# Where a decoder layer splits its experts' weights into fp16 halves

## The chip, the cores and the metric

One core of one Trainium2 chip runs the whole layer in a single launch. The metric is the device time of the launch in microseconds. The engines are PE (TensorE, with its weight loads as PEld), DVE (VectorE), ACT (ScalarE), POOL (GpSimd) and SP (SyncE, which here only issues DMAs).

## The reference, cut to what matters

```python
x = x + attn(layernorm(x))                  # x: 32 x 64 x 256; 16 heads of 16, ternary weights, activations quantized to int8
x = x + xattn(layernorm(x), ctx)            # 16 heads of 128; q and k go through an rmsnorm; ctx: 32 x 64 x 128
logits = xf @ router_w.T                    # 8 experts, the best 2 per token, softmax of the two
g = einsum('th,efh->etf', xf, gate_w)       # F = 688
u = einsum('th,efh->etf', xf, up_w)
y = einsum('etf,ehf->eth', silu(g) * u, down_w)
out = x + einsum('te,eth->th', combine, y)
```

The kernel multiplies fp32 numbers as pairs of fp16 numbers: a high half, and a low half that is what the high half leaves. Each product then is three fp16 products (high by high, high by low, low by high). The experts' weights (gate, up and down of 8 experts, 34304 fp32 columns on 128 partitions with padding) must be turned into such halves before the experts run. This splitting does not depend on the activations, so it can be done anywhere before them; the change moves it.

## The kernel before, in words

The kernel is four blocks in a row, with a barrier of all engines between them. Within a block every engine runs its own list of instructions in order, and semaphores tie the lists together. A wait holds everything behind it on its engine.

`self_attention` (L73) first normalizes, quantizes and transposes, then does 16 rounds, one for each tile of 128 tokens (`attention_rounds`, L139; the order within a round is the `attend` function of each engine, at L266 for ACT, L401 for DVE, L502 for PE). In round t ACT copies the turned probabilities out of PSUM (L270), copies q and k of tile t+3 (`highs`, L248), copies the values of tile t (`values`, L239), takes the exponentials of tile t+1 (L277), and at the end does `split(t + 2)` (L254): it scales one sixteenth of the experts' weights by 64 in place (L261) and rounds them to their high halves (L263, L264). DVE does `lows(t + 2)` (L362), `scores(t + 1)` (L369, with the subtraction of the maximum at L382), `sums(t)` (L384) and `outputs(t - 1)` (L392). PE does `probs` (L490), `project` (L454), `values` (L482), `scores` (L472) and `outputs` (L498). POOL subtracts to get the low halves (L203, L205). SP loads the next fp32 sixteenth and saves the finished halves to `gu_pair` and `d_pair` in DRAM (L163 to L184). Of the splitting, 16 pieces of 2144 columns are done, one per round, two of them ahead of round 0.

`attention_output` (L534) projects the result, and prepares the operands of the cross-attention: `hT` (the turned hidden states), `cT` (the turned context), `wq`, `wk`, `wvo`, `ck`.

`cross_attention` (L781) works on 4 groups of 512 tokens with 16 heads each, two heads per step: 32 pairs. It is written out step by step, `steps` N = -9 to 32 (L817). At step N the pair N+9 is projected (`query`, `key`, `squares`), the pair n = N+1 gets its scores and softmax, and pair N is attended and projected out. So steps -9 to -2 only project, steps -1 to 22 do all three, and the last steps, from N = 23, have no projection left. In a step, ACT's order is (L910 to L942): `out_high` of the odd head before (L893), `norm_logs` where a group opens, `query` (L882, L883), the copy of the turned probabilities pT (L922), the exponentials (L925), `key` (L889), `out_high` of the even head, `query` again, the cast of the probabilities (L937), `key` again. POOL's is (L860 to L874): multiply by the reciprocal sums (L869), multiply the next pair's norms (`both_norms`, L858), subtract for the low half of the probabilities (L874). PE turns that low half only when it is there (L1076). Where a group opens (n = 0, 8, 16, 24), ACT takes logs and exponentials of the norms (L897, L901, each with a load of its function table), SP writes them to DRAM and reads them back spread over the partitions in 16 DMAs (L847), and POOL and DVE wait for that. ACT issues no DMA in this block.

`experts` (L1160) routes the tokens, and runs 39 slots of 128 tokens on their experts, with the halves loaded back by SP (L1264, L1265). The loads of the first three experts are issued at its start, and those of the others once the routing is done.

Of the kernel before, what the change touches and what calls it, by code (L numbers as in the profile page):

```python
# [5 lines left out]
F32 = mybir.dt.float32  # L6
# [10 lines left out]
P = 128  # L17
# [51 lines left out]
GU, DH = NCH * FF, FT // 2 * C  # L69
CHUNK = GU + DH  # L70


def self_attention(nc, sem, dram, x_sb, cst, ao, arena):  # L73
# [4 lines left out]
    with ctx:  # L78
# [40 lines left out]

        raw = [arena[:, i * CHUNK:(i + 1) * CHUNK] for i in range(2)]  # L120
        pair = [arena[:, i * CHUNK:(i + 1) * CHUNK].bitcast(F16) for i in (2, 3)]
        raw_in = [sem(f"raw_in{i}") for i in range(2)]
        raw_zero, raw_scaled, pair_high, pair_low = sem("raw_zeroed"), sem("raw_scaled"), sem("pair_high"), sem("pair_low")
        pair_out = [sem(f"pair_out{i}") for i in range(2)]

# [28 lines left out]
        with nc.Block() as block:  # L154

            @block.sync
            def _(sp_):
# [5 lines left out]
                def load(e, g):  # L163
                    sp_.dma_start(raw[g][:, 0:GU], dram["wgu"][bass.ds(e, 1), g].rearrange("a p n -> (a p) n")).then_inc(raw_in[g], 16)
                    wd = dram["wd"][bass.ds(e, 1)]
                    full = 3 - g
                    sp_.dma_start(raw[g][:, GU:GU + full * C].rearrange("p (k o) -> p k o", o=C),
                                  wd[:, g * 3 * P:(g * 3 + full) * P, :].rearrange("a (k p) o -> p (a k) o", p=P)).then_inc(raw_in[g], 16)
                    if g:
                        sp_.dma_start(raw[g][0:FL, GU + 2 * C:GU + 3 * C], wd[:, (FT - 1) * P:FF, :].rearrange("a p o -> (a p) o")).then_inc(raw_in[g], 16)  # L170

                def save(e, g):
                    sp_.wait_ge(pair_low, e * 4 + 2 * g + 3)
                    sp_.dma_start(dram["gu_pair"][bass.ds(e, 1), :, g].rearrange("a p n -> (a p) n"), pair[g][:, 0:2 * GU]).then_inc(pair_out[g], 16)
                    sp_.dma_start(dram["d_pair"][bass.ds(e, 1), :, g].rearrange("a p n -> (a p) n"), pair[g][:, 2 * GU:2 * CHUNK]).then_inc(pair_out[g], 16)
                sp_.wait_ge(raw_zero, 1)
                load(0, 0)
                load(0, 1)
# [1486 lines left out]
```

## Time and profile before

| | us |
|---|---|
| device time, median of 3 runs | 1134.67 |
| lowest and highest of them | 1129.13, 1136.54 |
| the profiled execution, its device time | 1132.77 |
| its span, first to last instruction | 1131.0 |
| busy in the span: PE, DVE, ACT, POOL | 785.1, 674.0, 557.0, 342.8 |
| mean granted clock of PE, share of full | 0.877 |

The profiled execution is one of its own, 1.9 us below the median of the runs, and 1.8 us longer than its span. Matmul ends are modelled, and a share of busy time over the whole span mixes stages with different limits, so the rows below are read stage by stage.

### The profile page before, as it was taken

What the parts mean: (1) busy time and instruction counts of PE and PEld (TensorE: products, weight loads), DVE (VectorE), ACT (ScalarE), POOL (GpSimd) and SP (SyncE); (2) the same over time, 40 slices, a digit from 0 to 9 for tenths busy, and PEclk for the clock granted to TensorE, in tenths of its full rate; (3) what the DMA queues carried; (4) which work ended last, traced back from release to release, by engine and by line L of the source; (5) the groups of instructions that cost most, each with busy time, mean ns of one, the idle gap of its engine ahead of it and who ended that gap; (6) DMA issues with size and microseconds to landing.
All of it is one profiled execution on the core that took longest, in us unless ns stands there. A gap on an engine that the chain in (4) does not pass through costs nothing. (4 is left out here: it accounts for less than half of the span.)

```text
span 1131.0 us, 27058 instructions
## 1 busy us (share of the span) xinstructions
PE 785.1 (69%) x10378; PEld 562.7 (50%) x10379; DVE 674.0 (60%) x1178; ACT 557.0 (49%) x843; POOL 342.8 (30%) x375
## 2 busy tenths in 40 slices
PE   0015677752436769988997995665359999999993
PEld 0014666641322335655655664555346666666662
DVE  4996788869754557767776774546643333333330
ACT  0146899963733446555565654342124444444441
POOL 0301445532500013223232322330033444444442
PEclk9997776765758989998999997996569999999997
DMA  4002677648000020011002002007347222222223
GB/s 136 0 0 76 244 254 253 245 159 305 0 0 1 1 77 2 3 32 47 2 3 77 2 3 77 2 2 264 119 186 256 37 37 37 37 37 37 37 32 93
DMA packets 40062, 90.86 MB, mean 80 GB/s; under 512 B 5264, under 2 KB 25488, under 8 KB 38128
## 3 DMA queue, kind: packets, MB, share of 16 engines
q1 hardware_dynamic: 29168, 76.22, 19.0%
q0 software_dynamic: 7488, 10.23, 5.7%
q10 hardware_dynamic: 3328, 3.28, 0.8%
q8 instruction: 60, 0.98, 0.4%
q14 instruction: 18, 0.15, 0.0%
HBM read 62.71 MB, written 29.10 MB: 81 GB/s over the span
## 5 line engine op out<-in xcount | busy, mean ns | idle before, releaser
L1470 DVE SCALAR_TENSOR_TENSOR hid<-psu,hid 128x688 f32<-128x688 f32 x39 | 34.1, 874 | 168.4 <-ACT hid L1334 168.4
L1029 PE MATMUL xbank_q<-arena 128*128 128x512 f16 x384 | 97.7, 392 | 16.3 <-DVE q_hl L956 11.1
L1110 PE MATMUL xbank_a<-arena,x_o 128*128 128x256 f16 x768 | 96.2, 276 | 14.3 <-DVE x_o L966 14.3
L869 POOL TENSOR_TENSOR x_pf<-x_sc,x_rden 128x512 f32<-128x512 f32 x32 | 33.3, 1042 | 204.8 <-DVE x_rden L989 204.8
L1334 ACT ACTIVATE hid<-psg 128x688 f32<-128x688 f32 x39 | 29.0, 743 | 134.6 <-PE psu L1537 134.6
L1537 PE MATMUL psg<-wgu,f_xT 128*128 x468 | 76.6, 314 | 16.8 <-issue 10.9
L882 ACT ACTIVATE sqq<-xbank_q 128x512 f32<-128x512 f32 x64 | 38.2, 596 | 101.6 <-PE xbank_q L1029 101.6
L1551 PE MATMUL fbank<-arena,hidT 128*128 (+1 forms) x702 | 87.1, 273 | 1.5 <-ACT f_y L1352 0.8
L1110 PEld LDWEIGHTS xbank_a<-arena,x_o 128*128 128x128 f16 x768 | 73.0, 99 | 29.8 <-DVE x_o L966 21.2
L858 POOL TENSOR_TENSOR ao<-ao,rec_q 128x512 f32<-128x512 f32 x32 | 33.8, 1057 | 137.6 <-DMA ao<-key_norms 137.6
L1537 PE MATMUL psu<-wgu,f_xT 128*128 x468 | 75.0, 310 | 0.0
L956 DVE TENSOR_TENSOR q_hl<-xbank_q,q_hl 128x512 f16<-128x512 f32 x64 | 44.0, 687 | 47.4 <-ACT q_hl L883 47.4
L1551 PEld LDWEIGHTS fbank<-arena,hidT 128*128 128x128 f16 (+1 forms) x702 | 63.4, 97 | 16.9 <-issue 10.5
L203 POOL TENSOR_TENSOR arena<-arena 128x1376 f16<-128x1376 f32 x16 | 45.4, 2840 | 85.4 <-ACT arena L264 85.4
L1309 POOL DMA_INDIRECT token_out<-f_y,f_to x39 | 62.6, 1605 | 17.4 <-issue 17.0
L966 DVE SCALAR_TENSOR_TENSOR x_o<-xbank_o,x_o 128x512 f16<-128x512 f32 x64 | 43.9, 686 | 38.4 <-ACT x_o L893 38.3
L1537 PEld LDWEIGHTS psg<-wgu,f_xT 128*128 128x128 f16 x468 | 43.1, 99 | 47.0 <-issue 27.5
L1037 PE MATMUL xbank_k<-cT,wk 128*128 128x512 f16 x192 | 53.3, 388 | 12.9 <-DVE k_hl L962 12.9
L1029 PEld LDWEIGHTS xbank_q<-arena 128*128 128x128 f16 x384 | 33.0, 100 | 57.2 <-DVE q_hl L956 15.3
L893 ACT ACTIVATE x_o<-xbank_o 128x512 f16<-128x512 f32 x64 | 38.2, 597 | 40.4 <-PE xbank_o L1097 40.1
L1537 PEld LDWEIGHTS psu<-wgu,f_xT 128*128 128x128 f16 x468 | 46.0, 98 | 22.9
L960 DVE TENSOR_SCALAR k_hl<-xbank_k,x_gains 128x512 f16<-128x512 f32 x64 | 47.8, 747 | 10.7 <-ACT sqk L889 10.7
(278 smaller groups left out, 1932.0 us busy)
## 6 DMA issues: line engine op xcount, KB each, us to landing
arena<-in_wgu SPq DMA_DIRECT2D x16, 688.0 KB, 5.8
gu_pair<-arena SPq DMA_DIRECT2D x16, 688.0 KB, 3.1
wgu<-gu_pair SPq DMA_DIRECT2D x8, 1376.0 KB, 9.4
ao<-key_norms SPq DMA_DIRECT2D x64, 128.0 KB, 3.2
d_pair<-arena SPq DMA_DIRECT2D x16, 384.0 KB, 3.8
arena<-d_pair SPq DMA_DIRECT2D x8, 768.0 KB, 10.7
arena<-in_wd SPq DMA_DIRECT2D x8, 384.0 KB, 5.6
x_sb<-in_x SPq DMA_DIRECT2D x2, 1024.0 KB, 9.4
```

The source lines that it names most:

```text
L203: nc.gpsimd.tensor_tensor(pair[g][:, GU:2 * GU], raw[g][:, 0:GU], pair[g][:, 0:GU], ALU.subtract).then_inc(pair_low, 1)
L882: nc.scalar.activation(sqq[h % 2][:, :], bank_q[:, :], ACT.Square, scale=1.0 / (H_UP * W_UP)).then_inc(sq_done, 1)
L893: nc.scalar.mul(o_hl[h % 2][:, 0, :].rearrange("p (b n) -> p b n", b=2), ob[:, :, 0:RW], 1.0 / P_UP).then_inc(oh_done, 1)
L956: nc.vector.tensor_tensor(q_hl[:, 1, slot(h), :], bank_q[:, :], q_hl[:, 0, slot(h), :], ALU.subtract).then_inc(lq_done, 1)
L960: nc.vector.tensor_scalar(k_hl[:, 0, slot(h), :], bank_k[:, :], gains[:, 2:3], None, ALU.mult).then_inc(hk_done, 1)
L966: nc.vector.scalar_tensor_tensor(out=o_hl[h % 2][:, 1, :].rearrange("p (b n) -> p b n", b=2), in0=ob[:, :, 0:RW], scalar=1.0 / P_UP, in1=o ...
L1029: last = nc.tensor.matmul(bank_q[:, :], wq[:, a, k, f:f + D2], hT[:, b * NCH + k, at:at + GN], start=(j == 0), stop=(j == len(terms) - 1))
L1037: last = nc.tensor.matmul(bank_k[:, :], wk[:, a, f:f + D2], cT[:, b, at:at + GN], start=(j == 0), stop=(j == 2))
L1110: last = nc.tensor.matmul(acc[t // 2][:, (t % 2) * C:(t % 2 + 1) * C], o_hl[h % 2][:, a, at:at + P], wvo[:, b, e, :], start=(e == 0 and j ...
L1309: nc.gpsimd.indirect_dma_start(out=dram["token_out"], out_offset=bass.IndirectOffsetOnAxis(ap=to[:, 0:1], axis=0), in_=y[r ^ 1][:, :], in_ ...
L1537: last = nc.tensor.matmul(bank[:, c * 512:c * 512 + FH], xT[r][:, b * NCH + k, :], wgu[:, bass.ds(e, 1), at:at + FH].rearrange("p a n -> p ...
L1551: last = nc.tensor.matmul(ps[1][:, 0:C], hidT[r][0:rows, a, f, :], wd[0:rows, bass.ds(e, 1), at:at + C].rearrange("p a n -> p (a n)"), sta ...
```

## The change

The splitting is taken out of the self-attention rounds, of ACT, POOL and SP, and put into the steps of the cross-attention, on ACT and POOL. The weights now come in one array `wx` of 128 x 34304 fp32, in 67 pieces of 512 columns, two in each step from n = 0 to 33 (only one in the last). ACT itself issues the load of a piece (256 KB) and the save of its two halves (256 KB in 256 runs of 1 KB), where SP did before. ACT makes the high half in one operation straight from the fp32 piece (`piece_high`). POOL scales the piece in place, and subtracts (`piece_low`, two operations of 512 columns). There are two buffers: they lie in the parts of `hT` and `cT` that belong to group 0, which is why these two are laid out by group now, and why ACT issues the first two loads only at the end of step -2, when group 0 has been projected. `piece_save(i)` waits for POOL's low half, saves, and issues the load of piece i+2. At the end ACT waits for the last saves. The halves are kept in DRAM as one array `w_hl`, so the experts' loads read two runs per partition in place of one, with other offsets in `wgu` and `wd`. The copies to `hT` at L637 and L700 are written out in place of a loop.

```diff
@@ -66,8 +66,10 @@
 NE, FF = 8, 688
 FT = -(-FF // P)
 FL = FF - (FT - 1) * P
-GU, DH = NCH * FF, FT // 2 * C
-CHUNK = GU + DH
+GUC, DC = 2 * NCH * FF, FT * C
+EC = GUC + DC
+PIECE = 512
+NPIECE = NE * EC // PIECE
 
 
 def self_attention(nc, sem, dram, x_sb, cst, ao, arena):
...
-                def load(e, g):
...
-                def save(e, g):
-                    sp_.wait_ge(pair_low, e * 4 + 2 * g + 3)
...
-                with sp_.Fori(0, NE - 1) as e:
-                    for g in range(2):
-                        save(e, g)
-                        load(e + 1, g)
...
-                with pool.Fori(0, NE) as e:
-                    for g in range(2):
-                        pool.wait_ge(pair_high, e * 4 + 2 * g + 2)
...
-                        nc.gpsimd.tensor_tensor(pair[g][:, GU:2 * GU], raw[g][:, 0:GU], pair[g][:, 0:GU], ALU.subtract).then_inc(pair_low, 1)
...
-                        nc.gpsimd.tensor_tensor(pair[g][:, 2 * GU + DH:2 * CHUNK], raw[g][:, GU:CHUNK], pair[g][:, 2 * GU:2 * GU + DH], ALU.subtract).then_inc(pair_low, 1)
...
-                def split(t, r):
...
-                    act.wait_ge(raw_in[r], arrived)
...
-                    nc.scalar.mul(raw[r], raw[r], W_UP).then_inc(raw_scaled, 1)
-                    act.wait_ge(raw_scaled, t + 1)
-                    nc.scalar.copy(pair[r][:, 0:GU], raw[r][:, 0:GU]).then_inc(pair_high, 1)
-                    nc.scalar.copy(pair[r][:, 2 * GU:2 * GU + DH], raw[r][:, GU:CHUNK]).then_inc(pair_high, 1)
...
-                    if tile_there(t, 2):
-                        split(t + 2, r)
...
+        raw = [hT[:, 0].rearrange("p j n -> p (j n)").bitcast(F32)[:, i * PIECE:(i + 1) * PIECE] for i in range(2)]
+        pair_hl = [cT[:, 0], sb("x_pair", [P, 2, PIECE], F16)[:, :, :]]
+        raw_in, pair_out = [sem(f"x_raw_in{i}") for i in range(2)], [sem(f"x_pair_out{i}") for i in range(2)]
+        high_done, up_done, low_done = sem("x_pair_high"), sem("x_piece_up"), sem("x_pair_low")
         steps = range(-AHEAD, NPAIR + 1)
+
+        def piece(i):
+            return 0 <= i < NPIECE
 
         def pair(n):
             return 0 <= n < NPAIR
@@ -857,8 +808,17 @@
                     rq = rec_q[:, :, 2 * u:2 * u + 2].rearrange("p t h -> p h t").unsqueeze(3).to_broadcast([P, 2, GT, S])
                     nc.gpsimd.tensor_tensor(rk, rk, rq, ALU.mult).then_inc(rqk_done, 1)
 
+                def piece_low(i):
+                    r = i % 2
+                    pool.wait_ge(high_done, i + 1)
+                    nc.gpsimd.tensor_scalar(raw[r], raw[r], W_UP, None, ALU.mult).then_inc(up_done, 1)
+                    pool.wait_ge(up_done, i + 1)
+                    nc.gpsimd.tensor_tensor(pair_hl[r][:, 1, :], raw[r], pair_hl[r][:, 0, :], ALU.subtract).then_inc(low_done, 1)
+
                 for N in steps:
                     n = N + 1
+                    if piece(2 * n):
+                        piece_low(2 * n)
                     if opens(n):
                         both_norms(n)
                     if pair(n):
@@ -872,6 +832,8 @@
                         pool.wait_ge(ph_done, n + 1)
                         pool.wait_ge(pf_done, n + 1)
                         nc.gpsimd.tensor_tensor(p_hl[n % 2][:, 1, :], pf[:, :, :].rearrange("p a s -> p (a s)"), p_hl[n % 2][:, 0, :], ALU.subtract).then_inc(pl_done, 1)
+                    if piece(2 * n + 1):
+                        piece_low(2 * n + 1)
 
             @block.scalar
             def _(act):
@@ -906,11 +868,31 @@
                         act.wait_ge(rqk_done, g * NU)
                     nc.scalar.activation(rec_q[:, :, :].rearrange("p t h -> p (t h)"), bank_n[:, 2 * P:3 * P], ACT.Exp, scale=-0.5, bias=gains[:, 4:5]).then_inc(rq_done, 1)
 
+                def piece_load(i):
+                    act.dma_start(raw[i % 2], dram["wx"][:, i * PIECE:(i + 1) * PIECE]).then_inc(raw_in[i % 2], 16)
+
+                def piece_high(i):
+                    r = i % 2
+                    act.wait_ge(raw_in[r], (i // 2 + 1) * 16)
+                    if i >= 2:
+                        act.wait_ge(pair_out[r], i // 2 * 16)
+                    nc.scalar.mul(pair_hl[r][:, 0, :], raw[r], W_UP).then_inc(high_done, 1)
+
+                def piece_save(i):
+                    act.wait_ge(low_done, i + 1)
+                    act.dma_start(dram["w_hl"][:, :, i * PIECE:(i + 1) * PIECE].rearrange("l p n -> p l n"), pair_hl[i % 2]).then_inc(pair_out[i % 2], 16)
+                    if piece(i + 2):
+                        piece_load(i + 2)
+
                 act.wait_ge(g_ready, 4)
                 for N in steps:
                     n, m = N + 1, N + AHEAD
                     if head(2 * N - 1):
                         out_high(2 * N - 1)
+                    if piece(2 * n - 1):
+                        piece_save(2 * n - 1)
+                    if piece(2 * n):
+                        piece_high(2 * n)
                     if opens(n):
                         norm_logs(n // NU)
                     if pair(m):
@@ -927,6 +909,8 @@
                         key(2 * m)
                     if pair(N):
                         out_high(2 * N)
+                    if piece(2 * n):
+                        piece_save(2 * n)
                     if pair(m):
                         query(2 * m + 1)
                     if opens(n):
@@ -940,6 +924,18 @@
                     if opens(n):
                         act.wait_ge(pf_done, n + 1)
                         nc.scalar.copy(p_hl[n % 2][:, 0, :], pf[:, :, :].rearrange("p a s -> p (a s)")).then_inc(ph_done, 1)
+                    if piece(2 * n + 1):
+                        piece_high(2 * n + 1)
+                    if n == -1:
+
+                        act.wait_ge(q_done, H2)
+                        act.wait_ge(k_done, H2)
+                        for i in range(2):
+                            piece_load(i)
+                if piece(2 * NPAIR + 3):
+                    piece_save(2 * NPAIR + 3)
+                for r in range(2):
+                    act.wait_ge(pair_out[r], (NPIECE + 1 - r) // 2 * 16)
 
             @block.vector
             def _(dve):
...
-                    sp.dma_start(wgu[:, e, :], dram["gu_pair"][e].rearrange("p g n -> p (g n)")).then_inc(w_in[e % 2], 16)
-                    sp.dma_start(wd[:, e, :], dram["d_pair"][e].rearrange("p g n -> p (g n)")).then_inc(w_in[e % 2], 16)
+                    sp.dma_start(wgu[:, e, :].rearrange("p (l n) -> p l n", l=2), dram["w_hl"][:, :, e * EC:e * EC + GUC].rearrange("l p n -> p l n")).then_inc(w_in[e % 2], 16)
+                    sp.dma_start(wd[:, e, :].rearrange("p (l n) -> p l n", l=2), dram["w_hl"][:, :, e * EC + GUC:(e + 1) * EC].rearrange("l p n -> p l n")).then_inc(w_in[e % 2], 16)
...
```

## Rows read from the trace of the kernel before

**Rows 1.** Busy times by stretch, core 0: one round. Columns: stretch, length, PE, PEld, DVE, ACT, POOL busy, PE clock, DMA share, GB/s.
```profile
190.20:198.90 8.70, 7.27 (x124) 6.63 (x124) 7.17 (x12) 8.54 (x13) 4.42 (x3) 0.62 0.69 243
```

**Rows 2.** Timeline of ACT, one round: start us, duration us, line, operation.
```profile
183.21 1.97 ACT L261 ACTIVATE arena<-arena 128x2144 f32<-128x2144 f32 x1
...
187.31 1.07 ACT L270 COPY pT<-bank 128x512 f32<-128x512 f32 x2
...
191.93 1.97 ACT L261 ACTIVATE arena<-arena 128x2144 f32<-128x2144 f32 x1
```

**Rows 3.** Timelines of DVE and of PE in the same round.
```profile
189.48 0.75 DVE L365 SCALAR_TENSOR_TENSOR q_both<-bank,cst,q_sign 128x512 f16<-128x512 f32 x1 [1.28 <-ACT k_high L252]
...
190.90 1.92 PE L498 MATMUL bank<-vb,pT 128*64 128x32 f32 x32 [2.54 <-ACT vb L244]
...
192.76 1.97 PE L490 MATMUL bank<-cst,sp 128*128 128x128 f32 x8
```

**Rows 4.** Timeline of ACT: the copies that open rounds 0 and 1.
```profile
114.82 1.06 ACT L270 COPY pT<-bank 128x512 f32<-128x512 f32 x2
...
126.28 1.07 ACT L270 COPY pT<-bank 128x512 f32<-128x512 f32 x2
```

**Rows 5.** Timelines of ACT, PE and POOL: the middle of the cross-attention, two steps.
```profile
550.78 0.60 ACT L882 ACTIVATE sqq<-xbank_q 128x512 f32<-128x512 f32 x1 [2.25 <-PE xbank_q L1029]
...
561.55 0.60 ACT L882 ACTIVATE sqq<-xbank_q 128x512 f32<-128x512 f32 x1 [2.25 <-PE xbank_q L1029]
...
566.85 0.82 PE L1037 MATMUL xbank_k<-cT,wk 128*128 128x512 f16 x3 [0.49 <-DVE k_hl L962]
...
567.48 1.16 POOL L874 TENSOR_TENSOR x_p<-x_pf,x_p 128x512 f16<-128x512 f32 x1
```

**Rows 6.** DMA issues, timelines of ACT's and SP's queues (time to issue), and one landing.
```profile
1.28 0.60 ACTq L210 DMA_DIRECT2D w_raw<-in_wk  x1
...
113.06 0.39 SPq L174 DMA_DIRECT2D gu_pair<-arena  x1
...
114.16 0.88 SPq L164 DMA_DIRECT2D arena<-in_wgu  x1
...
ao<-key_norms SPq DMA_DIRECT2D x64, 128.0 KB, 3.2
```

**Rows 7.** Timelines of ACT and POOL where groups of heads open: groups 0 and 2.
```profile
403.71 1.28 ACT L897 ACT_TABLE_LOAD   x1
...
589.03 1.16 POOL L874 TENSOR_TENSOR x_p<-x_pf,x_p 128x512 f16<-128x512 f32 x1 [1.01 <-ACT x_p L937]
...
591.64 1.28 ACT L897 ACT_TABLE_LOAD   x1
...
609.02 1.15 POOL L874 TENSOR_TENSOR x_p<-x_pf,x_p 128x512 f16<-128x512 f32 x1
...
610.74 0.60 ACT L882 ACTIVATE sqq<-xbank_q 128x512 f32<-128x512 f32 x1 [1.54 <-PE xbank_q L1029]
```

**Rows 8.** Timelines of ACT and POOL: the last steps, with no projections left.
```profile
746.66 1.01 ACT L922 COPY x_pT<-xbank_s 128x1024 f16<-128x1024 f16 x1 [2.11 <-PE xbank_s L1084]
...
751.46 1.16 POOL L874 TENSOR_TENSOR x_p<-x_pf,x_p 128x512 f16<-128x512 f32 x1
...
754.70 1.01 ACT L922 COPY x_pT<-xbank_s 128x1024 f16<-128x1024 f16 x1 [2.11 <-PE xbank_s L1084]
...
759.25 1.15 POOL L874 TENSOR_TENSOR x_p<-x_pf,x_p 128x512 f16<-128x512 f32 x1 [0.73 <-ACT x_p L937]
...
761.12 1.01 ACT L922 COPY x_pT<-xbank_s 128x1024 f16<-128x1024 f16 x1 [0.49 <-PE xbank_s L1084]
```

**Rows 9.** Timelines of DVE and POOL: in the rounds, and at their end.
```profile
193.31 1.23 DVE L382 TENSOR_TENSOR sp<-sp,mx 128x1024 f32<-128x1024 f32 x1
...
233.92 1.64 POOL L205 TENSOR_TENSOR arena<-arena 128x768 f16<-128x768 f32 x1
...
234.17 2.48 DVE L382 TENSOR_TENSOR sp<-sp,mx 128x1024 f32<-128x1024 f32 x1
```

More of the change, by code:

```diff
@@ L161, in _ @@
                 sp_.dma_start(cst[:, :], dram["consts"]).then_inc(in_c, 16)
-                def load(e, g):
[L164 to L170, printed above, removed]
-                def save(e, g):
-                    sp_.wait_ge(pair_low, e * 4 + 2 * g + 3)
[L174 to L178, printed above, removed]
-                with sp_.Fori(0, NE - 1) as e:
-                    for g in range(2):
-                        save(e, g)
-                        load(e + 1, g)
-                for g in range(2):
-                    save(NE - 1, g)
-                for g in range(2):
-                    sp_.wait_ge(pair_out[g], NE * 32)
             @block.gpsimd
@@ L636, in _ @@
                 value_highs(4, H2 // 2)
-                with act.Fori(0, NT // 2) as i:
+                for i in range(NT // 2):
                     act.wait_ge(ht_done, i * 2 + 2)
-                    nc.scalar.copy(hT[:, :, bass.ds(i * 2 * P + P, P)], banks[1][:, :].bitcast(F16)[:, 0:4 * P].rearrange("p (j n) -> p j n", n=P)).then_inc(hT_ready, 1)
+                    nc.scalar.copy(hT[:, i // 2, :, (i % 2 * 2 + 1) * P:(i % 2 * 2 + 2) * P], banks[1][:, :].bitcast(F16)[:, 0:4 * P].rearrange("p (j n) -> p j n", n=P)).then_inc(hT_ready, 1)
             @block.vector
@@ L699, in _ @@
                 value_lows(4, H2 // 2)
-                with dve.Fori(0, NT // 2) as i:
+                for i in range(NT // 2):
                     dve.wait_ge(ht_done, i * 2 + 1)
-                    nc.vector.tensor_copy(hT[:, :, bass.ds(i * 2 * P, P)], banks[0][:, :].bitcast(F16)[:, 0:4 * P].rearrange("p (j n) -> p j n", n=P)).then_inc(hT_even, 1)
+                    nc.vector.tensor_copy(hT[:, i // 2, :, i % 2 * 2 * P:(i % 2 * 2 + 1) * P], banks[0][:, :].bitcast(F16)[:, 0:4 * P].rearrange("p (j n) -> p j n", n=P)).then_inc(hT_even, 1)
             @block.tensor
@@ L1025, in query @@
                         pe.wait_ge(lq_done, h)
[L1026 removed]
+                    f, g = h % H2 * D2, h // H2
                     terms = [(k, a, b) for k in range(NCH) for a, b in TERMS]
                     for j, (k, a, b) in enumerate(terms):
[L1029 removed]
+                        last = nc.tensor.matmul(bank_q[:, :], wq[:, a, k, f:f + D2], hT[:, g, b * NCH + k, :], start=(j == 0), stop=(j == len(terms) - 1))
                     last.then_inc(q_done, 1)
@@ L1034, in key @@
                         pe.wait_ge(lk_done, h)
-                    f, at = h % H2 * D2, h // H2 * GN
+                    f, g = h % H2 * D2, h // H2
                     for j, (a, b) in enumerate(TERMS):
-                        last = nc.tensor.matmul(bank_k[:, :], wk[:, a, f:f + D2], cT[:, b, at:at + GN], start=(j == 0), stop=(j == 2))
+                        last = nc.tensor.matmul(bank_k[:, :], wk[:, a, f:f + D2], cT[:, g, b, :], start=(j == 0), stop=(j == 2))
                     last.then_inc(k_done, 1)
```

41 lines of the change are left out of this document (13 added, 28 removed).

## The prediction, made before the change was run

> **What bounds the kernel now.** The page's slices come first: they show that the self-attention rounds, the cross-attention and the experts have limits of their own, so only the first two, which the change touches, are read closely. In a round the table by stretches has ACT busy 8.54 of 8.70 us and DVE 7.17 [rows 1]. The timeline of ACT says why: from one L261 to the next there are 8.72 us without a gap, and 4.10 us of them, 183.21 to 187.31, are the split [rows 2]. DVE waits 1.28 us a round for ACT, and PE 2.54 us [rows 3]. ACT bounds the rounds.
>
> The middle of the cross-attention is the reverse. A step is 10.77 us (550.78 to 561.55), ACT waits 2.25 us for PE before its first `query`, and PE itself waits only 0.49 us in the whole step, for DVE (L962) [rows 5]. That 0.49 us is the end of a chain: ACT's L882 and L883, pT, exponentials, DVE's sums and `key_halves`, PE's key. So PE has work all the time, and ACT's idle time there looks free; but whatever starts ACT's L882 later moves this chain and the step by as much. In the last steps, which have no projections, PE is no bound: a step is 8.04 us (746.66 to 754.70), a loop through pT, softmax and attention in which ACT waits 2.11 us for PE's transposes [rows 8]. Where a group opens, everything waits for ACT's logs of the norms and what follows them.
>
> **The rounds: what goes.** ACT's 4.10 us leave every round. What is late next is DVE: 8.72 less its wait of 1.28 is 7.44 us, and it is in order, so no round gets below that [rows 2, 3]. Close behind is a loop of PE and ACT: PE's projection, ACT's highs, values and exponentials (8.72 less the split's 4.10 and the copies' 1.0, so 3.6 us), PE's outputs (which need the values alone) and probabilities, and the projection again. At the half clock (1.2 GHz) outputs and probabilities cost 1.92 and 1.97 us [rows 3], and with a projection of about as much the loop is some 8.2 us; at 2.4 GHz PE's part about halves, and it is under 6.5 us. The clock in a round is now 0.62 of full [rows 1], so PE changes between the two levels, and idle time remains after the change. I take 7.9 us for a round, between 7.44 and 8.4. Rounds 1 to 13: 12 x 0.82 = 9.8 us. Round 0 lasts 11.46 us (114.82 to 126.28), as ACT stands waiting for a load, and becomes about 8: 3.4 us. pT of round 0 comes some 2.4 us sooner, as two splits stand ahead of it (one of them behind DVE's work). Rounds 13 and 14, with a late load and a DVE operation stretched from 1.23 to 2.48 us, give some 2.2 us [rows 4, 9]. Sum: 18 us, bounds 12 (8.4 us a round) and 23 (7.44).
>
> POOL's and SP's part of the rounds costs nothing now (both wait for ACT), and its going gains nothing. At the end of the block SP's last save lands ahead of DVE's last output.
>
> **The cross-attention: what comes.** Per piece ACT gets one operation, priced as its neighbours of 512 columns at 0.60 us (0.5 us to the next one's start), and two DMA issues, which stand in ACT's order. Issues take 0.60 us on ACT for 256 KB in 1 KB runs, and on SP 0.39 for a save and 0.88 for a load right behind one [rows 6]. I take 1.0 us for the two, bounds 0.78 and 1.76. POOL gets two operations: the subtraction is L874's, 1.16 us [rows 5]. A scaling of 512 fp32 columns by a constant stands in no row; below is half of L874's price, as it reads one stream in place of two, above is all of it. I take 0.9, nearer the top, as nothing shows that POOL gains much with one stream.
>
> As sums of busy time these fit in: 2 x (0.5 + 1.0) us on ACT, 2 x 2.1 us on POOL, in a step of 10.77 us. The order decides. The odd piece of a step goes so: ACT's high half at the step's end, POOL's `piece_low` behind L874, and at the head of the next step ACT stands still in `piece_save` until that is done. Behind this wait are the issues of save and load, the even piece's high half, and then all of ACT's step: `norm_logs`, `query`, pT, exponentials. Nothing of it needs the piece. From the end of L874 (or of the odd high, 0.2 us later) to the next ACT operation it is 0.15 us of semaphores + 0.9 + 1.15 + 1.0 + 0.5 = 3.7 us, bounds 3.1 and 4.7. I call it the pass, and compare it with what ACT has now at each place:
>
> - Full steps (18 that neither open a group nor follow an opening). L874 ends at 568.64, 7.09 us after L882; with the odd high 7.3, and with the pass the next L882 is 11.0 us after the last, where it is 10.77 now [rows 5]: 0.23 us a step, 4 us. It is nothing below a pass of 3.47.
> - Openings. For groups 1, 2 and 3 `norm_logs` starts at 591.64 (group 2 stands for all); L874 ends at 590.19, so it becomes 590.4 + 3.7 = 594.1 [rows 7]: 2.5 us, three times, 7.4 us. For group 0 it starts at 403.71, right behind the last key of step -2. Now two loads are issued there (0.9 us) and the first must land: 128 KB take 3.2 us from issue [rows 6], and the high half 0.5: 3.2 us later in all. Sum 10.6 us.
> - The step after each opening. For group 2 L874 ends at 610.17 and the next L882 starts at 610.74, only 0.57 us later: 3.1 us [rows 7]. The same sum at the other three gives 3.0, 2.4 and 2.2 us: 10.7 us.
> - The last steps. From pT to the end of L874 are 5.96 us (746.66 to 752.62); with the pass 9.66 us where it is 8.04 [rows 8]: 1.6 us, five times, and 0.3 in the first, which waits for DVE now. The last pT starts 0.7 us behind L874 (760.40 to 761.12) and now 3.7: 3.0 us more. The very last piece is rounded, subtracted, saved and landed before the block may end: some 2.4 us past the present end. Sum 13.8 us.
>
> Together 39 us. The save of the even piece waits too, but POOL has had over 3 us by then, so ACT doesn't stand. The loads have some 6 us to land: hidden. SP's DMAs of the norms meet at most two piece transfers of 256 KB: nothing, at most 1 us a group.
>
> By the Trainium skill, "GPSIMD Engine Reference", section 3.1, 512 elements of one stream take GpSimd 769 ns. That is not shown here; by it the pass is 3.57 us, and the sum 2 to 4 us smaller.
>
> **The experts.** The halves arrive in two runs per partition; no wait of PE on them stands high now, and the same bytes move: nothing, up to 1 us either way. Code written out for `hT`: nothing.
>
> **Sum.** 1132.77 - 18 + 39 = 1153.8 us for an execution like the profiled one, which is 1.9 us below the median of the runs; so 1155 us. The ends: pass 3.1 takes 14 x 0.6 + 4 = 12 off, with rounds at 7.44 that is 1133 - 23 + 27 = 1137; pass 4.7 puts 14 x 1.0 + 18 x 1.0 = 32 on, 1133 - 12 + 71 = 1192.
>
> **Rivals.**
> (A) Gain and cost even out: rounds bound by DVE and a short pass, 1137 us. For it: the 7.44 us are a firm floor and DVE's idle time is all ACT's doing; against it, PE's half clock [rows 1]. Chance 0.20.
> (B) Faster: ACT's stand at `piece_save` isn't on the chain, because PE, which is behind in its own list, catches up; only the loads ahead of group 0 (3.2), half of the other openings (3.7) and the last piece (2.4) cost: 1133 - 18 + 9 = 1124, and with DVE-bound rounds 1119. For it: PE waits only 0.49 us in a full step. Against it: the last steps, and the steps behind openings, where PE waits for ACT. Chance 0.12.
> (C) Much slower: POOL and DVE exclude each other. At 234.17 DVE's L382, which reads two SBUF tensors, took 2.48 us in place of 1.23, and ended 1.1 us after POOL's L205 (233.92 to 235.56) did [rows 9]: it stood until POOL was done. The cross-attention's subtraction of the maximum (L980) is of the same form, and the even piece's `piece_low` now starts at about its time. If it stands behind a POOL operation, 1.16 us less DVE's slack, say 0.8 us in 25 steps, is 20 us on top: 1175 us. Chance 0.10.
> The Trainium skill has this rule ("SBUF — State Buffer", on the shared port pair): such a DVE operation and a GpSimd operation that reads SBUF hold each other off for their full length. The trace agrees.
>
> **Chances.** The forecast has 0.58. A measurement of this kernel tells 1% (11 us) from no change. Slower by over 1%, above 1146: nearly all of the forecast and (C), 0.66; within 1%: (A), the forecast's low end and a third of (B), 0.26; faster: the rest of (B), 0.08. The range, 1135 to 1178, takes in (A) and (C) and leaves out (B) and the upper end.
>
> **What would show it.** Right: rounds of about 7.9 us with ACT idle in them; in the cross-attention ACT idle ahead of `piece_save`'s issues, released by POOL's subtraction; L882 at 11.0 us intervals; last steps of 9.7 us; `norm_logs` 2.5 us later against L874. The stretch of the rounds is 18 us shorter, the cross-attention 39 us longer. Wrong: full steps still at 10.77 us and last steps at 8.04 (then B), L980 drawn out (C), rounds at 7.44 (A), or issues well off 0.5 us each.

## The result, and the profile after

| | before | after |
|---|---|---|
| device time, median, us | 1132.85 | 1173.9 |
| runs, lowest to highest | 1129.13 to 1136.54 (4) | 1173.11 to 1174.72 (4) |
| the profiled execution's span | 1131.0 | 1172.6 |

After takes 1.0363 times as long as before, 95% interval 1.0324 to 1.0401: 41 us slower. (The runs of before taken beside the experiments have medians of 1131.2 to 1133.6.) Two runs in a slower state, one of before at 1451.7 us and one of e4 at 1974.6 us, are in the medians below and not in the ratios.

Where it went is read from busy times by stretch. The same four stretches of each kernel: the self-attention rounds (from PE's first projection to DVE's last output), what lies between, the cross-attention's block (to the point from which the experts' code runs), and the rest. Columns as in [rows 1]. First the kernel before:

```profile
96.50:251.70 155.20, 107.71 (x1984) 97.13 (x1984) 116.52 (x160) 138.66 (x193) 71.81 (x32) 0.70 0.59 210
251.70:343.60 91.90, 30.48 (x163) 22.15 (x164) 67.35 (x153) 41.64 (x40) 22.87 (x5) 0.59 0.26 96
343.60:771.20 427.60, 345.07 (x5700) 218.32 (x5700) 280.76 (x456) 219.90 (x372) 102.47 (x96) 0.96 0.08 22
771.20:1131.00 359.80, 289.34 (x2426) 215.20 (x2426) 131.15 (x257) 132.80 (x216) 136.34 (x236) 0.89 0.35 95
```

After:

```profile
98.90:230.00 131.10, 99.58 (x1984) 89.58 (x1984) 114.81 (x160) 76.17 (x145) 0.00 (x0) 0.73 0.01 1
230.00:321.30 91.30, 29.03 (x163) 21.33 (x164) 67.44 (x153) 41.53 (x40) 23.02 (x5) 0.61 0.26 96
321.30:816.50 495.20, 367.94 (x5700) 229.28 (x5700) 286.97 (x456) 253.07 (x439) 278.80 (x230) 0.90 0.30 90
816.50:1172.60 356.10, 286.77 (x2426) 214.48 (x2426) 131.23 (x257) 132.79 (x216) 135.64 (x236) 0.89 0.36 96
```

The rounds are 24.1 us shorter, the cross-attention 67.6 us longer; the start is 2.4 us longer (96.5 to 98.9), the stretch between 0.6 shorter and the rest 3.7 shorter: 2.4 - 24.1 - 0.6 + 67.6 - 3.7 = 41.6, the difference of the spans. No engine is full in the third row, the cross-attention: PE is busy 367.9 of 495.2 us, and POOL, which got most of the new work, 278.8. That points to an order rather than to a load; e1 tests it.

The timeline of DVE in the rounds of after:

```profile
132.48 0.75 DVE L309 SCALAR_TENSOR_TENSOR q_both<-bank,cst,q_sign 128x512 f16<-128x512 f32 x1
...
139.93 0.75 DVE L309 SCALAR_TENSOR_TENSOR q_both<-bank,cst,q_sign 128x512 f16<-128x512 f32 x1
```

L309 is L365 of [rows 3]. From 125.01 us on it waits for nothing in any round (no bracket), and a round is 7.45 us: DVE bounds it. The timeline of ACT, a full step of the cross-attention (L879 is `piece_high`, L883 the save, L872 the load, L844 the L882 of [rows 5], L904 the L922 of [rows 8]):

```profile
546.29 0.62 ACT L879 ACTIVATE x_pair<-arena 128x512 f16<-128x512 f32 x1
...
549.76 0.38 ACTq L883 DMA_DIRECT2D w_hl<-x_pair  x1
550.18 0.49 ACTq L872 DMA_DIRECT2D arena<-in_wx  x1
550.77 0.63 ACT L879 ACTIVATE cT<-arena 128x512 f16<-128x512 f32 x1 [2.60 <-issue]
551.30 0.58 ACT L844 ACTIVATE sqq<-xbank_q 128x512 f32<-128x512 f32 x1
...
552.25 1.02 ACT L904 COPY x_pT<-xbank_s 128x1024 f16<-128x1024 f16 x1
```

And POOL's timeline beside it (L834 is the L874 of [rows 5]; L814 is the scaling of a piece, L816 its subtraction):

```profile
545.54 1.16 POOL L834 TENSOR_TENSOR x_p<-x_pf,x_p 128x512 f16<-128x512 f32 x1
547.00 1.49 POOL L814 TENSOR_SCALAR arena<-arena 128x512 f32<-128x512 f32 x1 [0.30 <-ACT x_pair L879]
548.58 1.16 POOL L816 TENSOR_TENSOR x_pair<-arena,x_pair 128x512 f16<-128x512 f32 x1
```

Read the two together. POOL's L834 ends at 546.70; then 0.30 us of waiting, the scaling, 0.09, the subtraction until 549.74. ACT's save is issued at 549.76, so ACT had stood at `piece_save`; save, load, high half, and at 551.30 ACT takes up the step. The pass is 4.60 us, where the forecast had 3.7. The bracket on L879 says "issue": ACT's idle time is put down to the DMA issue in front, and it is the times of POOL that name the real releaser. In all, this idle time is large (97.2 us ahead of the even high halves), and POOL's scaling is the first of the page's costliest groups:

```profile
L814 POOL TENSOR_SCALAR arena<-arena 128x512 f32<-128x512 f32 x67 | 99.7, 1489 | 161.0 <-ACT cT L879 152.4
...
L879 ACT ACTIVATE cT<-arena 128x512 f16<-128x512 f32 x34 | 21.4, 630 | 97.2 <-issue 92.8
```

The granted clock of PE (the last column but two) is another thing that differs. Stretches from one copy of pT (L904) to the next: the first of all, a full one, the one behind the opening of group 2, and two of the last:

```profile
408.86:421.25 12.39, 11.31 (x175) 6.86 (x176) 8.71 (x14) 7.30 (x14) 8.50 (x8) 0.86 0.29 85
456.25:467.77 11.52, 10.34 (x180) 6.68 (x179) 8.61 (x14) 7.31 (x14) 8.46 (x8) 1.00 0.32 96
622.72:636.51 13.79, 12.71 (x178) 7.54 (x178) 9.81 (x16) 7.33 (x15) 8.52 (x8) 0.76 0.26 78
749.90:760.34 10.44, 6.51 (x118) 5.10 (x119) 4.42 (x8) 4.40 (x8) 8.42 (x7) 0.61 0.33 102
781.98:792.43 10.45, 7.21 (x135) 5.62 (x132) 4.75 (x9) 4.40 (x8) 8.42 (x7) 0.84 0.35 102
```

In the kernel before, the same places have a clock of 1.00. Where PE has a full list and the clock is below 1.00, PE is busy up to 2.4 us longer, and the step is longer too (12.39 and 13.79 us against 11.52); so a part of what is lost next to openings is likely the clock's. The full steps have 1.00, and the last steps are as long at 0.61 as at 0.84: neither is explained by it. No run was made to part clock and order at the openings.

### The profile page after: what moved, and what is told of

Same layout as the page of the kernel before. It is cut to its first block and busy times, and to the rows that moved or that the text cites. A ratio compares the mean times of both kernels' runs of the same rounds, so it can differ in the third digit from the quotient of the medians.

```text
span 1172.6 us, 27008 instructions
## 1 busy us (share of the span) xinstructions
PE 797.8 (68%) x10378; PEld 565.5 (48%) x10379; DVE 678.6 (58%) x1178; ACT 527.5 (45%) x862; POOL 446.4 (38%) x476
## 5 line engine op out<-in xcount | busy, mean ns | idle before, releaser
L814 POOL TENSOR_SCALAR arena<-arena 128x512 f32<-128x512 f32 x67 | 99.7, 1489 | 161.0 <-ACT cT L879 152.4
L1106 PE MATMUL xbank_a<-arena,x_o 128*128 128x256 f16 x768 | 105.6, 293 | 17.9 <-DVE x_o L962 17.9
L1025 PE MATMUL xbank_q<-arena 128*128 128x512 f16 x384 | 100.8, 402 | 15.3 <-DVE q_hl L952 10.4
L1106 PEld LDWEIGHTS xbank_a<-arena,x_o 128*128 128x128 f16 x768 | 77.6, 105 | 37.5 <-DVE x_o L962 24.4
L542 POOL TENSOR_TENSOR arena<-wq_raw,arena 128x2048 f16<-128x2048 f32 x2 | 10.8, 5411 | 214.6 <-ACT arena L551 214.4
L879 ACT ACTIVATE cT<-arena 128x512 f16<-128x512 f32 x34 | 21.4, 630 | 97.2 <-issue 92.8
L844 ACT ACTIVATE sqq<-xbank_q 128x512 f32<-128x512 f32 x64 | 37.8, 590 | 59.2 <-PE xbank_q L1025 54.0
L1093 PE MATMUL xbank_o<-x_pT,ck 64*128 64x64 f16 x1536 | 35.9, 197 | 29.9 <-ACT x_pT L904 29.9
```

What stands on the lines that cost most here:

```text
L814: nc.gpsimd.tensor_scalar(raw[r], raw[r], W_UP, None, ALU.mult).then_inc(up_done, 1)
L844: nc.scalar.activation(sqq[h % 2][:, :], bank_q[:, :], ACT.Square, scale=1.0 / (H_UP * W_UP)).then_inc(sq_done, 1)
L1025: last = nc.tensor.matmul(bank_q[:, :], wq[:, a, k, f:f + D2], hT[:, g, b * NCH + k, :], start=(j == 0), stop=(j == len(terms) - 1))
L1093: last = nc.tensor.matmul(ob[:, half, at:at + S], ck[rows, l, h // H2 * 2 + a, b * CC:(b + 1) * CC], pT[rows, h % 2, m, a, b * S:b * S + S ...
L1106: last = nc.tensor.matmul(acc[t // 2][:, (t % 2) * C:(t % 2 + 1) * C], o_hl[h % 2][:, a, at:at + P], wvo[:, b, e, :], start=(e == 0 and j ...
```

## The experiments

The kernels e1, e2, e3, e4 and e8 are the changed kernel with one edit; e5 and e6 are e4 with one more, e7 is e6 with one more, and e9 is e7 with one more. Times are medians; "ratio" is to the kernel before run beside it. The last four columns are read off ACT's timelines, from the starts of pT's copies (L904 of after): the first of them; a full step; the three steps around the openings of groups 1, 2 and 3, the nine summed; and from the seventh pT before the end to the last one, six steps. Each is read in the one profiled execution of its kernel; e7's took 1125.4 us, above its other four runs (1116.6 to 1119.4). For before and after the same readings stand ahead.

| | time, us | ratio, 95% interval | first pT | full step | nine steps at openings | last six |
|---|---|---|---|---|---|---|
| before | 1132.85 | | 424.07 | 10.77 | 118.1 | 46.6 |
| after | 1173.9 | 1.036 | 408.86 | 11.52, some 11.94 | 144.2 | 63.0 |
| e1_save_late | 1134.12 | 0.9993 [0.997, 1.0017] | 405.72 | 10.77 | 129.3 | 54.5 |
| e2_no_scale | 1136.61 | 1.0022 [0.9994, 1.005] | 406.56 | 10.77 | 131.7 | 53.5 |
| e3_no_pieces | 1105.58 | 0.974 [0.9704, 0.9777] | 399.07 | 10.77 | 115.6 | 46.7 |
| e4_sp_queue | 1132.78 | 1.0004 [0.9975, 1.0033] | 403.68 | 10.77 | 128.9 | 52.4 |
| e5_issues_only | 1139.59 | 1.0073 [1.0047, 1.0098] | 405.78 | 10.77 | 132.7 | 56.8 |
| e6_tables_apart | 1133.27 | 1.0008 [0.9983, 1.0033] | 405.24 | 10.77 | 130.9 | 52.2 |
| e7_scale_moved | 1118.82 | 0.987 [0.9845, 0.9895] | 407.03 | 10.77 | 126.6 | 48.2 |
| e8_scale_twice | 1269.12 | 1.1209 [1.1145, 1.1272] | 409.44 | 14.3 to 15.0 | 164.2 | 81.2 |
| e9_table_first | 1113.4 | 0.9829 [0.9792, 0.9865] | 401.17 | 10.77 | 122.3 | 47.9 |

**e1: the wait moved, all work kept.**

```diff
-                    if piece(2 * n - 1):
-                        piece_save(2 * n - 1)
                     if piece(2 * n):
                         piece_high(2 * n)
...
                         nc.scalar.activation(sc[n % 2][:, :, :], sc[n % 2][:, :, :], ACT.Exp).then_inc(exp_done, 1)
+                    if piece(2 * n - 1):
+                        piece_save(2 * n - 1)
                     if pair(m):
                         key(2 * m)
```

> ScalarE's step of the cross-attention no longer begins with the save of the odd piece: its wait for GpSimd's subtraction and the two DMA issues behind it stand after the exponentials, before the first key's square. Every instruction stays, and the bytes. If the wait at the head of the step is the cost (the theory): the full steps fall back from 11.5 to 12.0 us to near the 10.8 us of the kernel before, the steps around the group openings and the last seven lose 1 to 3 us each, and the time is 1132 to 1152 us. If the cost is the load itself (GpSimd's 177 us of work, its port with VectorE, or the traffic of the pieces), the order changes nothing: 1168 to 1176 us. If the two issues and the high half on ScalarE are the cost, also 1165 us or more.

1134.1 us: 40 of the 41 us are gone, with every instruction and byte still there. ACT's timeline in the middle:

```profile
536.02 1.01 ACT L902 COPY x_pT<-xbank_s 128x1024 f16<-128x1024 f16 x1
536.03 0.38 ACTq L883 DMA_DIRECT2D w_hl<-x_pair  x1
...
543.35 0.62 ACT L879 ACTIVATE cT<-arena 128x512 f16<-128x512 f32 x1
545.71 0.60 ACT L844 ACTIVATE sqq<-xbank_q 128x512 f32<-128x512 f32 x1 [1.73 <-PE xbank_q L1025]
```

The step's first operation waits for PE again, as in [rows 5]: the order was the cost of those 40 us, and the amount of work as such was not. It doesn't make the pieces free: nine steps at openings and the last six are still 11 and 8 us above the kernel before.

**e2: the scaling left out.**

```diff
-                    nc.gpsimd.tensor_scalar(raw[r], raw[r], W_UP, None, ALU.mult).then_inc(up_done, 1)
-                    pool.wait_ge(up_done, i + 1)
```

> GpSimd's multiplication of each piece by the scale is left out (67 of 1.49 us), so the low halves are those of unscaled weights; all else is as after. If the wait at the head of the step is the cost, each step whose pass is on the chain shortens by up to 1.49 us: the full steps only by their excess of about 0.75 us (20 of them, 15 us), openings and the steps behind them and the last seven by 1.5 us (some 14 of them, 21 us): 1130 to 1145 us. If VectorE's exclusion by GpSimd's two-input operations is the cost, nothing is won, since the multiplication has one input: 1168 us or more. If the DMA issues or the traffic are the cost: 1168 us or more.

1136.6 us, in the range of the first theory: the same 37 to 40 us, though the wait stays at the head of the step. Two edits that each take most of the cost can't both be its whole cause; e5 and e8 sort that out.

**e3: no pieces.** SyncE writes a constant tile in the places of the halves instead.

```diff
-NPIECE = NE * EC // PIECE
+NPIECE = 0
...
+                    for i in range(g * 17, min(g * 17 + 17, NE * EC // PIECE)):
+                        sp.dma_start(dram["w_hl"][:, :, i * PIECE:(i + 1) * PIECE].rearrange("l p n -> p l n"), pair_hl[1]).then_inc(pair_out[0], 16)
```

> No piece is loaded, split or waited for in the cross-attention; SyncE writes a constant tile to the place of the halves, 67 saves of 256 KB in four lots behind each group's norm tables (so the experts compute with constants, and the bytes of the saves stay). If all that the pieces cost is ScalarE's passes, GpSimd's work and the loads, the cross-attention takes the 428 us of the kernel before again, and the rounds keep their gain of 24 us: 1104 to 1112 us. If the traffic of the saves disturbs the steps, more than 1115 us.

1105.6 us: as expected. With the pieces gone altogether the kernel is 27 us faster than before (1132.9 - 1105.6), some 25 of them in the stretch of the rounds, and the pieces cost 68 us in the cross-attention (1173.9 - 1105.6). The last steps are at 8.04 us again, and the traffic of 67 saves disturbs nothing that can be seen.

**e4: loads and saves through SyncE's queue.** ScalarE keeps the high halves; SyncE waits for GpSimd in its place.

```diff
-                    act.wait_ge(low_done, i + 1)
-                    act.dma_start(dram["w_hl"][:, :, i * PIECE:(i + 1) * PIECE].rearrange("l p n -> p l n"), pair_hl[i % 2]).then_inc(pair_out[i % 2], 16)
...
+                    sp.wait_ge(low_done, i + 1)
+                    sp.dma_start(dram["w_hl"][:, :, i * PIECE:(i + 1) * PIECE].rearrange("l p n -> p l n"), pair_hl[i % 2]).then_inc(pair_out[i % 2], 16)
```

> All loads and saves of the pieces are issued by SyncE's queue, which waits for GpSimd's subtraction in ScalarE's place; at a group's opening they stand before and behind the norm tables as ScalarE had them. ScalarE keeps the high halves alone. If the wait at the head of the step is the cost: gone with the issues, 1.7 us of ScalarE's time per step as well, so at or below the kernel with the later save: 1120 to 1145 us. If the cost is GpSimd's work or the traffic: 1168 us or more. A rival inside the theory: the high half at the head of the step now waits for its load, since GpSimd reaches the odd piece late; then the time is between, 1145 to 1165 us.

1132.8 us, no better than e1 within its interval, though ScalarE has 1.7 us less to do in a step: once the wait is off the head, the issues cost nothing in full steps, and 2 us in the last six together. The openings show something new. SP's timeline:

```profile
480.34 1.72 SPq L813 DMA_DIRECT2D key_norms<-x_kc  x4
483.10 11.00 SPq L819 DMA_DIRECT2D ao<-key_norms  x16
494.14 0.59 SPq L795 DMA_DIRECT2D w_hl<-cT  x1
```

The even piece's save stands behind 16 table loads for 11 us, and with it the next load.

**e5: the issues alone taken from ScalarE; its wait stays at the head.** On top of e4:

```diff
+                    if piece(2 * n - 1):
+                        act.wait_ge(low_done, 2 * n)
                     if piece(2 * n):
                         piece_high(2 * n)
```

> SyncE issues all loads and saves, as in the run before, but ScalarE still waits for GpSimd's subtraction of the odd piece at the head of its step, and issues nothing there. What goes from ScalarE's pass is the two issues alone, 0.38 and 0.49 us, twice per step; the wait itself stays. By the prediction's sum (the issues are 1.0 us of a pass whose wait is the rest) the time falls from 1173.9 us by up to 0.9 us in each of some 34 steps, less where the step has room: 1143 to 1160 us. If the wait for GpSimd is all of the cost: 1168 us or more, since SyncE sets off the next load no sooner. If the issues are all of it: 1130 to 1136 us.

1139.6 us, somewhat below the 1143 to 1160 of the prediction's sum, and far from the 1168 of "the wait is all of it". Timeline of ACT, a full step and two last steps (L899 is the high half, L918 the copy of pT):

```profile
548.51 0.63 ACT L899 ACTIVATE cT<-arena 128x512 f16<-128x512 f32 x1 [1.60 <-POOL x_pair L839]
...
741.04 0.99 ACT L918 COPY x_pT<-xbank_s 128x1024 f16<-128x1024 f16 x1
...
750.49 0.99 ACT L918 COPY x_pT<-xbank_s 128x1024 f16<-128x1024 f16 x1
```

ScalarE still stands for GpSimd at the head of the step (1.60 us), and yet the full step is 10.77 us. The last step is 9.45 us where it was 10.45 (in after's timeline 792.43 - 781.98 = 10.45): 1.0 less, just the two issues (549.76 to 550.77 above). So there is one loop: pT, exponentials, DVE's sums, POOL's halves, ACT's odd high half, scaling, subtraction, save, load, even high half, first query, pT. In a full step it measured 11.52 us, and without it a full step takes the 10.77 us of the kernel before (PE busy for 10.28 of them, as in every run with such steps), so a full step has an excess of only 0.75 us, 12.7 us over the fifteen that lie clear of openings; any edit that takes 0.75 off the loop (the issues 1.0, the scaling 1.57 with its gap, the wait altogether) takes all of it. That is why e1, e2 and e5 won much the same, 40, 37 and 34 us, with edits of different size. In the last steps, where PE is no bound, they differ: 9.45 with the issues gone, 8.6 in e2 (737.90 to 746.52 in its timeline), 8.35 to 10.28 in e1.

**e8: the scaling done twice.** By 8 and by 8; the same numbers come out.

```diff
-                    nc.gpsimd.tensor_scalar(raw[r], raw[r], W_UP, None, ALU.mult).then_inc(up_done, 1)
-                    pool.wait_ge(up_done, i + 1)
+                    nc.gpsimd.tensor_scalar(raw[r], raw[r], W_UP ** 0.5, None, ALU.mult).then_inc(up_done, 1)
+                    pool.wait_ge(up_done, 2 * i + 1)
+                    nc.gpsimd.tensor_scalar(raw[r], raw[r], W_UP ** 0.5, None, ALU.mult).then_inc(up_done, 1)
+                    pool.wait_ge(up_done, 2 * i + 2)
```

> As the changed kernel, but GpSimd scales each piece in two operations, by 8 and again by 8 (the same numbers come out): 1.49 us more per piece, some 1.57 with the gap behind it. If the steps run on one loop from the transposed probabilities over the exponentials, GpSimd's halves, the odd piece's scaling and subtraction, the two issues and the next step's first operations, all of it is paid in every step now, since none has room left: full steps 11.5 to 13.1 us, last steps 10.4 to 12.0 us, 34 steps x 1.57 = 53 us, the time 1220 to 1235 us. If GpSimd's time in bulk is the cost (67 pieces x 1.57 = 105 us), or a part of it runs beside the chain, it ends elsewhere: at 1260 us or more, or under 1205 us.

1269.1 us: 95 us more, where one pass per step gives 53 and all of the work 105. The expectation was wrong. POOL's timelines say why; e8, a last step:

```profile
812.26 1.15 POOL L818 TENSOR_TENSOR cT<-arena,cT 128x512 f16<-128x512 f32 x1
813.37 1.04 POOL L831 TENSOR_TENSOR x_pf<-x_sc,x_rden 128x512 f32<-128x512 f32 x1
```

And after, a full step and a last one:

```profile
541.54 1.16 POOL L816 TENSOR_TENSOR cT<-arena,cT 128x512 f16<-128x512 f32 x1
543.52 1.04 POOL L829 TENSOR_TENSOR x_pf<-x_sc,x_rden 128x512 f32<-128x512 f32 x1 [0.83 <-DVE x_rden L985]
...
783.74 1.15 POOL L816 TENSOR_TENSOR cT<-arena,cT 128x512 f16<-128x512 f32 x1
784.99 1.04 POOL L829 TENSOR_TENSOR x_pf<-x_sc,x_rden 128x512 f32<-128x512 f32 x1
```

The even piece is scaled and subtracted ahead of L829, the product that the softmax waits for. In the full steps of after it left 0.83 us; in the last steps none (no bracket). So the even piece is on the loop as well as soon as it grows: last steps rose from 10.45 to 13.58 us (808.93 to 822.51 between pT's copies), 3.13, which is 2 x 1.57, and full steps from 11.52 to 14.31 at least, 2.79. By this reading 1.57 of the 2.79 are the odd piece and 0.74 the even one (1.57 less the 0.83 it had left). The remaining 0.5 and what some steps have above 14.31 weren't tried apart; in e8 DVE's subtraction of the maximum takes 1.26 to 1.69 us in ten of the steps with projections, where after has 0.69 in its full steps, and the clock is 0.77 to 0.89 in most full steps. The changed kernel stood closer to the edge than the forecast said.

**e6: the tables kept apart (an edit of e4).** The even save and next load are issued between the norm table's save and its loads; the even high half comes behind the norms.

```diff
+                    piece_save(2 * n)
                     sp.wait_ge(kc_saved, (g + 1) * GT * 16)
```

> As the run with SyncE's queue, with the opening mended in two places: the save of the even piece and the next load are issued between the norm tables' save and their loads (not behind 16 loads of 11 us), and ScalarE's even high half at an opening stands behind the norms. The openings there took 12.5, 18.9 and 13.5 us for the steps around it, against 12.0, 16.2 and 12.0 without pieces. If the late load at the opening is what is left of them: 2 to 4 us less per group, 1119 to 1128 us. If GpSimd's work is what is left, 1130 us or more.

1133.3 us: the gain of 2 to 4 us a group did not come. SP's timeline has the reason:

```profile
481.12 1.73 SPq L813 DMA_DIRECT2D key_norms<-x_kc  x4
485.69 0.38 SPq L795 DMA_DIRECT2D w_hl<-cT  x1
486.49 0.35 SPq L791 DMA_DIRECT2D arena<-in_wx  x1
486.96 10.03 SPq L820 DMA_DIRECT2D ao<-key_norms  x16
```

The save must wait for GpSimd's subtraction (it ends at 485.66), and the tables stand behind it: they start 5.8 us behind the save of the norms, 2.8 in e4. One stall in the queue was exchanged for another.

**e7: the split dealt out anew (on top of e6).** ScalarE scales in place, VectorE copies the high half, GpSimd only subtracts.

```diff
-                    nc.scalar.mul(pair_hl[r][:, 0, :], raw[r], W_UP).then_inc(high_done, 1)
+                    nc.scalar.mul(raw[r], raw[r], W_UP).then_inc(up_done, 1)
...
+                    nc.vector.tensor_copy(pair_hl[r][:, 0, :], raw[r]).then_inc(high_done, 1)
```

> As the run with the tables apart, and the split is dealt out anew: ScalarE scales the piece in place (in place of its high half, one operation of the same size), VectorE makes the high half by a copy of 128x512 (new: 67 of at most 0.7 us), and GpSimd only subtracts (67 of 1.16 us; its 67 multiplications of 1.49 us are gone). The result is the same. If GpSimd's time is what the last steps and openings still pay (8 to 10 us where 8.0 are possible): 1108 to 1120 us, the 1105.6 us without pieces being the floor. If VectorE's copies delay the chain more than GpSimd's multiplications did: 1125 to 1140 us.

1118.8 us, within the range expected if GpSimd's time is what was still paid, 1.3% faster than before and 4.7% faster than after: the last six steps are 4 us shorter than in e6, the nine at openings as well. In the profiled executions e7 is 7.8 us ahead of e6; the medians differ by 14.5, more than these steps show.

**e9: the first table ahead (on top of e7).**

```diff
-                    piece_save(2 * n)
                     sp.wait_ge(kc_saved, (g + 1) * GT * 16)
...
+                        if u == 0:
+                            piece_save(2 * n)
```

> As the run with the scaling moved, but at an opening SyncE issues the first unit's two table loads before the save of the even piece, which there waited for GpSimd until 485.97 us and held the tables' loads back to 488.22, 5.7 us behind the norm save's issue at 482.53. If that is what the openings still pay (18.7, 17.5 and 19.0 us against 16.2, 15.0 and 16.1 without pieces): 1.5 to 2.5 us less for each of the three later groups, 1111 to 1116 us. If not, 1117 to 1121 us.

1113.4 us, as expected: 1.7% faster than before and 5.2% faster than after. Against e7 the intervals of the two ratios overlap by a little, so the 5 us between the medians rest on the trace too: the nine steps are 4.3 us shorter. SP's timeline, to hold against e6's:

```profile
476.67 1.72 SPq L813 DMA_DIRECT2D key_norms<-x_kc  x4
479.44 1.09 SPq L819 DMA_DIRECT2D ao<-key_norms  x2
480.58 1.40 SPq L795 DMA_DIRECT2D w_hl<-cT  x1
482.03 0.47 SPq L791 DMA_DIRECT2D arena<-in_wx  x1
482.54 9.90 SPq L819 DMA_DIRECT2D ao<-key_norms  x14
```

The first table, which alone is needed soon, starts 2.8 us behind the norms' save. The e9 kernel keeps the whole split and computes what the others do; it is 8 us from the kernel without pieces.

## Why the prediction was right, step by step

The forecast was 1155 us and slower by over 1%, with the range to 1178; it came to 1173.9. The sign and the mechanism held; sizes were off on both sides, and here the errors took from each other: the rounds gained 6 us more than was forecast, the cross-attention lost 29 us more. That the time still lies in the range is luck in part, since the range reached to 1178 for the sake of (C), whose mechanism turned out small.

- **The rounds, -18: measured -24.1.** The mis-sized term is the choice of 7.9 us for a round, between the floor of 7.44 and 8.4 for the loop of PE and ACT. DVE's rounds are 7.45 us with no wait: the floor, to 0.01 us, and the loop through PE did not bound them. A faster PE isn't shown: the granted clock of the stretch went from 0.70 to 0.73, and the outputs of single rounds took from 1.12 to 1.92 us before as well as after; the 1.92 of [rows 3] was the slow end. In the round at 141.17 outputs and probabilities took 1.90 and 1.88 us, but the projection 1.06, and the round was 7.47 us long: there the three were not slow together, as the 8.2 us of the loop supposed. Of rival (A) the half on the rounds was right. The rounds of e3 are some 25 us shorter than before's as well.
- **The cross-attention, +39: measured +67.6.** The mechanism is shown: e1 moves the stand at `piece_save` alone, and 40 us go. The mis-sized term is the pass, 4.60 us and not 3.7. Of these 0.9 us, 0.59 are the scaling (1.49 against 0.9, outside the bound of 1.16), some 0.25 the gaps ahead of POOL's two operations, and the issues came as forecast (549.76 to 550.77, 1.01 us). With the forecast's own slope, where a pass longer by 1.0 us adds 32 us, 0.9 adds 29: 39 + 29 = 68 us, against 67.6. So close a fit is luck in part: by this sum full steps would be 11.9 us and are 11.52, and the openings and last steps, where the clock fell too, cost more than it says and make up for it. The 1.16 had been taken as the upper bound since one stream should not cost more than two; it did.
- **Full steps at 11.0 us:** 11.52, and 11.9 in three, in each of which a load's issue took 1.4 us in place of 0.49. 0.23 us of excess became 0.75 and more: a small error in the pass triples a term that is the difference of two large ones. The fifteen that lie clear of openings cost 12.7 us.
- **Openings:** group 0's `norm_logs` came 2.8 us later against the start of the block (3.2 forecast), and the first pT 7.1 us later: 0.9 more lie between `norm_logs` and the exponentials, and 3.4 in the step behind the opening (2.2 to 3.1 forecast for such steps). The nine steps at the other three cost 26.1 us (144.2 - 118.1), where the forecast has some 16.
- **Last steps at 9.66:** 10.45, which is 9.66 and the 0.9 of the pass, less 0.1. The last pT and the tail together: from 761.12 to the block's end at 771.2 before, from 802.63 to 816.5 after, 3.8 us more.
- **"POOL has had over 3 us by then, so ACT doesn't stand" at the even save:** barely true in full steps (the subtraction ends at 542.70, the save is issued at 542.73), and no longer in the last ones, where ACT stands from 784.20 to 784.92 and POOL's L829 starts right behind the even subtraction. e8 shows what it costs once that piece grows.
- **"I take 1.0 us for the two" issues:** right as a size. As for its worth, e4 against e1 gives nothing once they are off the loop, and e5 gives 34 us for the same issues while they are on it.
- **(A), even out (1137):** refuted by the pass. **(B), not on the chain:** refuted by e1 and by the 10.45 us steps.
- **(C), POOL and DVE exclude each other:** its time, 1175, is what was measured, but not for its reason. The subtraction of the maximum (L976 here) has

```profile
L976 DVE TENSOR_TENSOR x_sc<-x_sc,x_mx 128x512 f32<-128x512 f32 x32 | 26.0, 813 | 1.1
```

 0.81 us in the mean, where the kernel before has 0.69: 4 us in 32 steps, where (C) put 20. The mechanism is there (1.63 us in the step behind each opening of groups 1, 2 and 3), but small. And e1, with the same 0.8 us in the mean (26.4 us in 32), is 40 us faster than after.
- **The clock.** The forecast had no term for PE's clock in the cross-attention, where the kernel before has 0.96 in the mean and after 0.90. How much of the openings' cost it is stays open.
- **The rest.** The start was 2.4 us longer and the experts 3.7 us shorter, both taken as nothing. The start's code is the same in after and all experiments, and yet DVE's first L309 lies between 98.75 and 102.70 us in their profiles (98.92 before, 101.28 after), so the 2.4 us show nothing. The experts' stretch is 0.7 to 3.7 us shorter than before's in after, e1 to e7 and e9; why stays open.

## What to carry to other kernels

When work is handed to an engine "that has room", look for the one instruction that waits in an in-order queue, and move the wait before moving the work: here the same instructions cost 68 us with the wait at the head of the step, and 28 with it half a step later. A loop that exceeds another bound by little answers to any small relief as if that relief were the whole cause, so the gains of single edits (40, 37 and 34 us) neither add up nor name the culprit; stretches where the other bound is absent, as the last steps here, tell the edits apart. And a queue shared by two streams, as SP's at the openings, needs its order by need, first table first.

## What the runs showed of the hardware

- GpSimd's multiplication of 128x512 fp32 by a constant, in place, took 1.49 us each time, longer than its subtraction of two such tiles, 1.16 us. The Trainium skill's "GPSIMD Engine Reference", section 3.1, has 769 ns for 512 elements as the best case of a tight loop; this multiplication took nearly twice that, and the measurement decides.
- VectorE's copy of 128x512 from fp32 to fp16 in e9 took 0.42 us as a rule, but 1.20 us in most of the last steps and behind the openings, where it met an operation of GpSimd. DVE's and then POOL's timelines of e9:

```profile
725.54 1.20 DVE L995 CAST x_pair<-arena 128x512 f16<-128x512 f32 x1 [1.75 <-ACT arena L895]
...
729.30 0.42 DVE L995 CAST cT<-arena 128x512 f16<-128x512 f32 x1
```

```profile
725.30 1.15 POOL L855 TENSOR_TENSOR x_p<-x_pf,x_p 128x512 f16<-128x512 f32 x1
```

 POOL's operation ended at 726.45, the copy 0.29 us later, which fits a copy that stood for most of that time. So a stretch like the 2.48 us of [rows 9] is met with a VectorE operation of one input, too. No run was made for it alone.
- The issue of a 256 KB load took 0.46 to 0.50 us as a rule and 0.6 to 1.7 us in 12 of after's 67, and it varied alike on SP's queue in e9 (up to 1.49). In after, for one:

```profile
554.66 1.38 ACTq L872 DMA_DIRECT2D arena<-in_wx  x1
```

 What stretches it was not tried.
